# Two bf16 casts of a message go from DVE to ACT in the second convolution of a graph network

## The reference, cut to what matters

```python
def _gcn_conv(x, row, col, edge_w, W, b, num_nodes):
    ...
    deg = jax.ops.segment_sum(ew, c, num_segments=num_nodes)
    dis = jnp.where(deg > 0, jax.lax.rsqrt(deg), 0.0)
    norm = dis[r] * ew * dis[c]
    xw = x @ W.T
    msg = xw[r] * norm[:, None]
    out = jax.ops.segment_sum(msg, c, num_segments=num_nodes)
    return out + b
```

## Time and profile before

| | |
|---|---|
| median of three executions | 16107.46 us |
| the three executions | 16124.14, 16107.46, 16105.67 us |
| the profiled execution: its span, first to last instruction | 16116.0 us |
| the profiled execution's own device time | not recorded apart from the three above; its span lies between them |
| busy share of the span: PE, DVE, ACT, POOL | 78%, 60%, 19%, 72% |
| mean granted clock of TensorE | 0.733 |
| the `g2` pass, 403 batches, within the span | about 4500 to 7310 us |

### The profile page before, as it was taken

How to read it: one execution, slowest core, us unless ns; L and a number is a source line. 1 busy time by engine, 2 the same in 40 slices (tenths; PEclk the granted TensorE clock), 3 DMA queues, 4 the chain that set the end, 5 groups by cost and what they waited for, 6 DMA issues and landing times. The chain is left out here.

```text
span 16116.0 us, 333728 instructions
## 1 busy us (share of the span) xinstructions
PE 12602.6 (78%) x95144; PEld 10233.5 (63%) x95144; DVE 9628.8 (60%) x29955; ACT 3020.2 (19%) x5120; POOL 11677.0 (72%) x12296
## 2 busy tenths in 40 slices
PE   3888888888689999996777777777667777777775
PEld 2666666666489999994555555555545555565554
DVE  5444544544488888886555555555565555555555
ACT  1333333333200000001111111111121111111111
POOL 5777777777776666665777777777667777777775
PEclk5555555555599999996888888888777777777776
DMA  3222222222221111112556566555545555555552
GB/s 114 69 69 70 69 69 69 69 69 69 66 40 30 29 30 29 30 29 70 170 170 172 169 173 171 170 170 170 145 121 143 144 144 144 143 145 146 143 144 72
DMA packets 1973695, 1714.55 MB, mean 106 GB/s; under 512 B 1266475, under 2 KB 1436319, under 8 KB 1972431
## 3 DMA queue, kind: packets, MB, share of 16 engines
q10 hardware_dynamic: 939256, 958.97, 18.4%
q0 software_dynamic: 394560, 282.16, 10.8%
q1 hardware_dynamic: 639488, 469.70, 10.2%
HBM read 1096.56 MB, written 615.90 MB: 106 GB/s over the span
## 5 line engine op out<-in xcount | busy, mean ns | idle before, releaser
L814 POOL DMA_INDIRECT s_gt<-ta_d,s_ix x6448 | 6109.1, 947 | 2082.8 <-issue 1932.1
L814 POOL DMA_INDIRECT g_gt<-xs_d,g_ix x3224 | 3048.4, 946 | 1022.5 <-issue 982.4
L687 DVE TENSOR_TENSOR s_P<-psw,dlT 128x1024 f32<-128x1024 f32 x806 | 985.3, 1222 | 2842.2 <-PE psw L1057 2833.3
L1010 PE MATMUL pair<-g_part,g_Oh 128*128 128x224 bf16 x25389 | 2499.8, 259 | 100.8 <-DVE g_sel L846 63.8
L814 POOL DMA_INDIRECT g_gt<-ys_d,g_ix x2015 | 1924.5, 955 | 879.3 <-issue 507.7
L1010 PEld LDWEIGHTS pair<-g_part,g_Oh 128*128 128x128 bf16 x25389 | 2406.7, 98 | 129.6 <-issue 105.6
L1057 PEld LDWEIGHTS psw<-s_R,s_P 128*128 128x128 f32 x12896 | 1932.3, 228 | 629.6 <-issue 629.6
L1035 PE MATMUL pair<-ident,s_gt 128*128 128x128 f32 x3224 | 709.9, 360 | 2066.3 <-DMA s_gt<-ta_d,s_ix 2065.0
L1035 PEld LDWEIGHTS pair<-ident,s_gt 128*128 128x128 f32 x3224 | 460.9, 180 | 2300.4 <-issue 1337.9
L1057 PE MATMUL psw<-s_R,s_P 128*128 128x64 f32 x12896 | 1836.5, 305 | 2.1 <-DVE s_R L922 1.3
L1057 PEld LDWEIGHTS psw<-g_R,g_P 128*128 128x128 f32 x6448 | 1398.8, 329 | 607.4 <-issue 607.4
(11 more groups left out here) (333 smaller groups left out, 16270.1 us busy)
## 6 DMA issues: line engine op xcount, KB each, us to landing
s_dl<-dl_d SPq DMA_DIRECT2D x404, 512.0 KB
seg_d<-s_sg ACTq DMA_DIRECT2D x806, 256.0 KB
s_Bw<-tb_d ACTq DMA_DIRECT2D x3224, 48.0 KB
s_Bw<-tb_d SPq DMA_DIRECT2D x3224, 48.0 KB
seg_d<-g_sg ACTq DMA_DIRECT2D x403, 320.0 KB
z_d<-g_rT ACTq DMA_DIRECT2D x403, 256.0 KB
s_z<-z_d ACTq DMA_DIRECT2D x403, 256.0 KB
s_gt<-ta_d,s_ix POOLq DMA_INDIRECT x6448
```

The source lines that it names most:

```text
L687: return eng.tensor_tensor(P[:, :, :], bc(columns.rearrange("p (o e) -> p o e", o=1), [128, G, 128]), bc(dlT[:, bass.ds(j * G, G)].rearran ...
L814: eng.indirect_dma_start(out=gt[k][:, s, :], out_offset=None, in_=table[:, :], in_offset=bass.IndirectOffsetOnAxis(ap=ix[k][:, s:s + 1], a ...
L1010: last = eng.matmul(near_out(k, t), Oh[k][:, g, 128 * t:128 * t + 128], part[n][:, g, :, :].rearrange("p f l -> p (f l)"), start=g == 0 an ...
```

## The change: what it does

In the `g2` pass DVE no longer makes the two casts. It signals `v_msr` when `R` is made. ACT makes the first cast (`R` into part 0) at the head of its step, and the second cast (`rest` into part 1) at the end of its step, behind the evacuation and the store. DVE makes `P`, waits for the first cast (`a_c0`), subtracts, makes the `Oh` of batch j-3, waits for the second cast (`a_c1`), and makes the last subtraction, which signals `v_msg`. The three drains between the parts and the one before them are gone. The other three passes have the same instructions as before, and so has PE in all of them.

```diff
--- before.py
+++ after.py
@@ -694,6 +694,7 @@
+        v_msr, a_c0, v_rest, a_c1 = [mark(f"e_{n}") for n in ("vmsr", "ac0", "vrest", "ac1")]
...
@@ -852,16 +853,6 @@
-                    def message_parts(eng, k):
-
-                        eng.tensor_copy(Rp[k][:, :, 0, :], R[k][:, :, :])
-                        eng.drain()
-                        eng.tensor_tensor(rest[:, :, :], R[k][:, :, :], Rp[k][:, :, 0, :], ALU.subtract)
-                        eng.drain()
-                        eng.tensor_copy(Rp[k][:, :, 1, :], rest[:, :, :])
-                        eng.drain()
-                        return eng.tensor_tensor(Rp[k][:, :, 2, :], rest[:, :, :], Rp[k][:, :, 1, :], ALU.subtract)
-
...
@@ -883,15 +874,6 @@
-                        if stage(j, L_PT) and held is not None:
-                            t = b - L_PT
-                            h = (t // 2) % 2
-                            eng.wait_ge(s_dl[h].sem, (i * 2 + t // 4 + 1) * 16 + s_dl[h].base)
-                            done(eng, p_u, j, L_PT + 2)
-                            for g in range(GN):
-                                last = eng.tensor_scalar(Oh[t % 2][:, g, :], dl[h][:, t % 2 * xp * 128:(t % 2 + 1) * xp * 128],
-                                                         iog[:, g:g + 1], None, ALU.is_equal)
-                            last.then_inc(v_pt.sem, 1)
...
@@ -902,13 +884,13 @@
-                                if thin:
-                                    eng.drain()
-                                    last = message_parts(eng, k)
-                                last.then_inc(v_msg.sem, 1)
+                                last.then_inc((v_msr if thin else v_msg).sem, 1)
                         if stage(j, L_LN):
                             k = (b - L_LN) % 2
                             onehot(eng, P[k], columns, j - L_LN).then_inc(v_p.sem, 1)
+                            if thin:
+                                done(eng, a_c0, j, L_LN)
+                                eng.tensor_tensor(rest[:, :, :], R[k][:, :, :], Rp[k][:, :, 0, :], ALU.subtract).then_inc(v_rest.sem, 1)
...
@@ -922,6 +904,19 @@
+                        if stage(j, L_PT) and held is not None:
...
+                            for g in range(GN):
+                                last = eng.tensor_scalar(Oh[t % 2][:, g, :], dl[h][:, t % 2 * xp * 128:(t % 2 + 1) * xp * 128],
+                                                         iog[:, g:g + 1], None, ALU.is_equal)
+                            last.then_inc(v_pt.sem, 1)
+                        if stage(j, L_LN) and thin:
+                            k = (b - L_LN) % 2
+                            done(eng, a_c1, j, L_LN)
+                            eng.tensor_tensor(Rp[k][:, :, 2, :], rest[:, :, :], Rp[k][:, :, 1, :], ALU.subtract).then_inc(v_msg.sem, 1)
...
@@ -942,6 +937,10 @@
                     def step(j, i, b):
+                        if stage(j, L_LN) and thin:
+                            k = (b - L_LN) % 2
+                            done(eng, v_msr, j, L_LN)
+                            eng.activation(Rp[k][:, :, 0, :], R[k][:, :, :], ACT.Copy).then_inc(a_c0.sem, 1)
...
@@ -989,6 +988,10 @@
+                        if stage(j, L_LN) and thin:
+                            k = (b - L_LN) % 2
+                            done(eng, v_rest, j, L_LN)
+                            eng.activation(Rp[k][:, :, 1, :], rest[:, :, :], ACT.Copy).then_inc(a_c1.sem, 1)
                     drive(eng, step, L_DONE)
```

More of the change, by code:

```diff
@@ L924, in step @@
                                                   ALU.mult).then_inc(v_ln.sem, 1)
+                        if stage(j, L_PT) and held is not None:
+                            t = b - L_PT
+                            h = (t // 2) % 2
+                            eng.wait_ge(s_dl[h].sem, (i * 2 + t // 4 + 1) * 16 + s_dl[h].base)
+                            done(eng, p_u, j, L_PT + 2)
+                            for g in range(GN):
[6 more added lines that the diff above has]
+                            eng.tensor_tensor(Rp[k][:, :, 2, :], rest[:, :, :], Rp[k][:, :, 1, :], ALU.subtract).then_inc(v_msg.sem, 1)
                     drive(eng, step, L_SUM if mlp and summed else L_LN)
@@ L1102, in edge_loop @@
                     v_msg.passed(NIST)
+                for m in (v_msr, a_c0, v_rest, a_c1) if thin else ():
+                    m.passed(NIST)
                 if near:
```

## The result

The changed kernel took **16154.78 us**, the median of eight executions (16150.98 to 16156.49), against 16108.42 us for the kernel before in eight executions beside it: + 46 us, a ratio of 1.0028 with a 95% interval of 1.0018 to 1.0038. It is slower, by a little more than the 0.2% that counts as no change, though the interval's lower end lies just inside it. The forecast was 16159 us. Of the executions reported further down one, of e3b_onehots_head, took 19347 us in the slow state, against 15991 to 15997 us in its three others; its ratio is made without it.

What follows compares the result with a forecast made beforehand. A closed two-batch loop through ACT's evacuation and second cast was to bind the `g2` pass: 14.26 us, 7.13 per batch against 6.996, + 0.13 x 400 = + 52 us on 16107, giving 16159 us; range 16100 to 16235.

Steps and rivals of the forecast that it cites:

- DVE's gain of 0.9 us per batch: Casts and drains leaving DVE take 0.94 us per batch, about 0.05 comes back; its own path falls to about 6.1 us.
- The loop's sum, 14.26 us: Evacuation, store's issue, cast, last subtraction, DVE's work up to `Oh`, fetch, next evacuation: 14.26 us for two batches, 7.13 each.
- the gap from the store's issue to the cast: On ACT, from the end of the store's DMA issue to the next instruction, the second cast: 0.11 us.
- the hand-over of ACT to DVE: From ACT's second cast to DVE's last subtraction: 0.10 us taken, at least 0.06.
- `Oh` to the fetch: Hand-over from DVE's one-hots to PE's fetch: 0.10 us taken, at least 0.06.
- the seven one-hots: DVE's seven `Oh` instructions per batch, part of the two-batch loop: 1.87 us.
- the indices to the pick: On DVE behind the last subtraction, from the indices to the pick: 0.07 us.
- the cast: ACT's cast of 128 columns from SBUF: 0.31 us; a second figure of 0.41 us was weighed and set aside.
- Rival A: DVE's sequencer prepares nothing past the new wait: 0.25 us more, loop 14.51, 7.26 per batch, + 104 us; chance 0.20.
- Rival B: The loop does not bind and PE sets the pace at 6.8 us per batch: - 78 us; chance 0.10.
- Rival C: Store's issue overlaps ACT's cast, loop about DVE's old path: 13.81, - 36 us, or half, 14.03, + 8 us; chance 0.13.
- Rival D: PE idles more and the clock falls to the lower level in this pass: + 2400 us; chance 0.02.

Runs made afterwards that it cites:

- e3b_onehots_head: Changed kernel with DVE's one-hots back at the head of its step, second ACT cast still behind evacuation and store; 15996.20 us, ratio 0.9928 to the kernel before.
- e1b: Changed kernel with ACT's second cast moved right behind the first, ahead of evacuation and store; 15991.30 us, ratio 0.9926 to the kernel before.
- e2b: Changed kernel with ACT's second cast between the evacuation and the store's issue; 16070.57 us, ratio 0.9975 to the kernel before.
- e4: Kernel before, casts on DVE with drains, only the one-hots moved behind `P`; disturbed job, 22511 us against 22523, ratio 1.001.
- e8: Changed kernel with the second cast back on DVE before the last subtraction, with one drain; disturbed job, 23078 us against 22882, ratio 1.0086.
- e7: Changed kernel with an extra 128-column ACT copy between the first cast and the evacuation; disturbed job, 22772 us against 22882, ratio 0.9951.
- e1: Changed kernel with ACT's second cast right behind the first, ahead of evacuation and store; disturbed job, 22942 us against 22523, ratio 1.0189.
- e6: Changed kernel with second cast ahead of the evacuation and one-hots at the head of DVE's step; disturbed job, 22962 us against 22882, ratio 1.0038.
- e2: Changed kernel with ACT's second cast between evacuation and store's issue; disturbed job, 22423 us against 22523, ratio 0.9958.
- e3: Changed kernel with DVE's one-hots back at the head of its step; disturbed job, 22422 us against 22523, ratio 0.9957.
- e4b: Kernel before with only the one-hots moved behind `P`, run again; disturbed job, 22621 us against 22882, ratio 0.9876.
- e5: Changed kernel with one more 128-column ACT copy between the store's issue and the second cast; 16193.97 us, ratio 1.0052 to the kernel before.

## Why the prediction was right

Time and direction were right, 16159 forecast and 16155 measured, and the mechanism is the one named: a loop over two batches through the evacuation, with PE waiting for the one-hots at its end. The size of the effect was less close than the time: + 52 us forecast, + 46 between the medians, + 38 between the two profiled passes (0.134 us per batch forecast, 0.094 measured). By its own steps:

- **DVE's gain of 0.9 us per batch** was there: with the loop open, DVE waits for PE at every pick (e1b).
- **The loop's sum, 14.26 us.** Measured 14.03 in a plain stretch and 14.15 (2 x 7.075) with the turns. The loop is 0.11 us shorter than the sum, and single terms were off in both directions. Too long: the gap from the store's issue to the cast (0.05, not 0.11, from 6445.84 + 0.34 to 6446.23), the hand-over of ACT to DVE (6446.57 - 6446.54 = 0.03, not 0.10), `Oh` to the fetch (0.05, not 0.10), and the seven one-hots, 136.5 / 79 = 1.73 us, not 1.87. Too short: the indices to the pick, 0.07 to 0.24 and 0.15 on average where I had 0.07. Right: the cast, 0.31 as worked out from the two copies of 512 columns; the estimate of 0.41 that I worked out from the Trainium skill (ScalarE: Activation LUTs, Rules for kernel authors) was 0.1 too long here. The page gives its 0.3 us per ACTIVATE for one whose bias is a pointer operand, and these copies have none, so the figure was not one for them.
- **Rival A** was true as a mechanism. The sequencer does stand still at the wait, in the changed kernel and in e1b. The price came at other places than A had it: its sign, indices over 0.3 us behind the subtraction, shows only at the loop turns, which cost 0.43 us once in eight batches, and the pick starts 0.07 to 0.24 us behind the indices (before, the one-hots followed them 0.07 behind). The turns lengthen the two-batch loop by 14.15 - 14.03 = 0.12 us on average, and with some 0.1 at the pick that is near the 0.25 that A asked for. A's time, + 104 us, did not come, since other terms of the sum were too long by as much. The Trainium skill (Perfetto Trace Analysis, DVE / Act Engine Instruction) lets the sequencer go on at once; at this wait the traces disagree (0.045 to 0.047 us behind the cast's end at each of 92 turns), and I should not have taken its rule against A without a row.
- **Rival B** did not happen in this kernel, but its price is real once the loop is opened, and larger than I said: PE's own pace is 6.66 us, not 6.8, so opening it gave - 121 us and not - 78. I had taken PE's busy time per batch, 6.77 us, for a floor; the ends of matmuls that it counts up to are modelled by the profile, and the start-to-start of PE's own work was the better figure (6.657 us with no idle time in e1b).
- **Rival C** asked for an overlap of the store's issue with the cast. There is none, the gap between them is 0.05 us (e2b shows what it would have been worth).
- **Rival D** did not happen, the granted clock stayed at 1.00.

That the forecast came out within 4 us of the measurement is partly luck: terms too long by 0.06 + 0.07 + 0.05 + 0.14 = 0.32 us stand against some 0.2 us that I had left out. And the 14 us by which the forecast lay above the growth of the profiled pass were partly hidden by the 8 us by which the profiled execution of the kernel before ran over its median.

What stays open: whether moving the one-hots alone, without ACT, is free (e4), whether the first cast alone brings the whole gain (e8), and the control with the extra copy outside the loop (e7). In the disturbed jobs e1, e6 and e8 were slower than the kernel before, e2, e3, e4b and e7 faster, and e4 the same; why is not shown.

## What to carry to other kernels

When work is handed to an idle engine, that engine's share of busy time does not say what it costs; look at what stands in front of it in that engine's order, and follow the chain from there until it comes back to itself. Here one cast behind an instruction that waited for PE, and one-hots behind the wait for that cast, closed a loop over two batches; its length over two was the period, to within a tenth of a microsecond, and each microsecond put in or taken out counted half. Open such a loop at either end before giving up the change: the same casts on the same engine gave 16155 us behind the evacuation and **15991 us ahead of it**, with e3b (15996) the fastest of this study and some 120 us under the kernel before.

## What the runs showed of the hardware

A DVE instruction that waits for another engine held up DVE's sequencer too: in the changed kernel and in e1b the loop's end began 0.045 to 0.047 us behind the end of ACT's cast at each of 92 turns, even where the engine itself was still busy with earlier work. Of two ACT copies of 128 columns in a row, 0.31 and 0.29 us long, the second started 0.22 us behind the first (e5). And one program ran 40% slower in two of three jobs (16112 against 22523 and 22882 us), with PE standing still for about 0.4 to 1.3 us at a time and no wait in the profile that would explain it; the jobs ran on three chips, and whether the chip makes the difference is not shown. A comparison made there cannot tell anything of a pass that is bound by a few tenths of a microsecond elsewhere.
